# Expert weights that come turned, split beside the first experts, and bias rows made ahead of the last queries

## The chip, the cores and the metric

One core of a Trainium2 chip runs the whole kernel. The metric is device time in microseconds, the median of several executions. TensorE (PE) multiplies and transposes, VectorE (DVE), ScalarE (ACT) and GpSimd (POOL) work on elements, SyncE (SP) issues most transfers. Each engine takes its own instructions in order and waits on semaphores for the others.

## What is computed

Four batches of 512 rows of 128 go through two layers, with a residual after each part:

```python
x = x + L0_xattn(ctx, ctx, layernorm(x))      # 16 heads, features exp(z), exp(-z), 77 keys
x = x + L0_ffn(layernorm(x))                  # 8 experts of 64, top 2 of 8, and a shared one
x = x + L1_xattn(layernorm(x), ctx, ctx, mask)   # one head of 128, masked softmax over 77 keys
x = x + L1_ffn(layernorm(x))                  # 8 experts of 512, top 2, gelu(gate) * up, down
```

In the last part `gu = einsum('th,efh->etf', x, gate_up_w)` with `gate_up_w` of shape (8, 1024, 128) and `out = einsum('etf,ehf->eth', h, down_w)` with `down_w` of shape (8, 128, 512). TensorE needs both with the contracted index on the partitions, so turned against the way they are stored.

## The kernel before, in words

Everything stays in SBUF between the parts. Tokens lie 128 to a tile, four tiles to a batch. The order of work is written out by hand for each engine; semaphores carry the counts.

**First attention.** A step `G` (0 to 15) is one batch and a group of four heads: `scores(G)` on TensorE, `Exp` on ScalarE (L1013), `values`, a transposition, `normalise` on DVE. Beside it run the maxima of the next batch: GpSimd rounds the queries into `qh` (`round_queries`, L386), TensorE multiplies them with `kb`, DVE reduces (`mx`, L573). The negated maxima are transposed, copied by ScalarE (`copy_mT0`, L959, for batch 0 into `mT0`; `copy_mT`, L963, into `mT`) and moved by SP into `qs` (L310, L314). `project(b)` multiplies the output of batch b with `fc_w` and adds a bias row through `onecol` and `b2s`, for which it waits on `pool_bias`. GpSimd builds these rows (L410 to L429: the selection `selGt` and `selG`, the zeroed gates `g3`, the bias split in `b2p`, `b2s`, `onecol`) after `round_queries(3, q)`.

**First experts.** `hidden(b, c)`, c = 0 to 4, makes four parts of the expert layer and the shared layer of batch b; ScalarE applies Gelu (L1043), `spread_gates` spreads the gates, DVE multiplies (`gated`, L692), `moe_out` sums into banks 5 and 6, DVE adds the residual and takes the statistics (L697, L516, L519). The gates: `gate_logits`, `gate_exp`, then on DVE `gate_scores`, `first_best`, `second_best`, `best_weights`, `gate_parts` (ends at L627), then `turn_gates` on TensorE and `copy_gates` (L684). Batch 0 and batch 1 have gates of their own, batches 2 and 3 one chain together. A normalisation is `layernorm_stats`, `layernorm_rstd` on GpSimd (L364, L365) and `layernorm_apply` (L528).

**Second attention.** `scores1(b)`, `softmax_shift` on DVE (L748, L751, L754), `softmax_exp` (L1070), `turn_probs`, `copy_probs` (L1084), `values1`, `attention1_out` on DVE (L767 to L770 and statistics), a normalisation, `turn_xn3`, `expert_logits`. It starts after `moe_out(3)`. Between these, the weights of the second experts are turned: for each expert SP loads `upn` and `dnn` (L323, L324; the first three when the first attention is over, the rest as the ring of three comes free), `turn_weights(e)` transposes 12 blocks (L1507) into three banks, ScalarE copies two into `uphi`, rounded for a fast multiply, and one into `dnT` (L1066), and DVE subtracts the rounded part from the bank into `uplo` (`low_weights`, L762).

**Second experts.** Routing, then 39 blocks of 128 rows in a loop: a gathered block is multiplied with `uphi`, `uplo` and again `uphi` (L1139), Gelu, product, transposition, `down`. TensorE waits for `dve_upT` before it.

Of the kernel before, what the change touches and what calls it, by code (L numbers as in the profile page):

```python
# [16 lines left out]
P = 128  # L17
# [10 lines left out]
WR = 3  # L28
# [45 lines left out]
def two_layer_kernel(nc, A, out):  # L74
    with ExitStack() as ctx:
# [54 lines left out]
        g3 = sb("g3", [P, NT, 3, GR], BF16)  # L130
        g3r = sb("g3r", [P, NT, E0])


        l0 = ExitStack()
# [19 lines left out]
        mT0 = sb("mT0", [GH, NG, SEQ], at=l0)  # L154
        selGt = sb("selGt", [3 * E0, 3, 4 * P], BF16, at=l0)
# [29 lines left out]
        upn = sb("upn", [P, WR, 8, D])  # L185
        dnn = sb("dnn", [P, WR, F1])
        uphi = sb("uphi", [P, E1 * 2 * F1], F32R)
        uplo = sb("uplo", [P, E1 * 2 * F1], F32R)
# [39 lines left out]
        XT2 = (0, 1, 7, 1)  # L228
        XT3 = (5, 5, 5, 1)
        UPT = (2, 3, 0)  # L230
# [27 lines left out]
        pe_upT, act_upT, dve_upT = sem("pe_upT"), sem("act_upT"), sem("dve_upT")  # L258
# [31 lines left out]
        def _(sp):  # L290
# [16 lines left out]

            for g in range(NG):
# [8 lines left out]
            sp.wait_ge(dve_on, STEPS)  # L317
            sp.wait_ge(act_onT, NB * NI)
            sp.wait_ge(pool_mask, 1)
            for e in range(E1):  # L320
                if e >= WR:
                    sp.wait_ge(pe_upT, 3 * (e - WR + 1))
                sp.dma_start(upn[:, e % WR, :, :], A["L1_ffn_gate_up_w"][e].rearrange("(c f) h -> f c h", f=P)).then_inc(ld_up[e], 16)  # L323
                sp.dma_start(dnn[:, e % WR, :], A["L1_ffn_down_w"][e]).then_inc(ld_dn[e], 16)  # L324

# [20 lines left out]
        def _(g):  # L346
# [59 lines left out]
            for q in range(NG):  # L406
                round_queries(3, q)
# [17 lines left out]
            for t in range(3):  # L425
# [4 lines left out]
                .then_inc(pool_bias, 1)  # L430
            g.wait_ge(ld_mask, 16 * NB)
# [71 lines left out]
        def _(v):  # L503
# [178 lines left out]
            def copy_gates(b):  # L682
                v.wait_ge(pe_gT, b + 1)
                v.tensor_copy(gT3[:, b, :], bank[7 if b else 5].bitcast(BF16)[0:BR, 0:SEQ]).then_inc(dve_gT, 1)  # L684
# [15 lines left out]

            normalise(STEPS - 2)
# [15 lines left out]
            layernorm_apply(1, 3)  # L717
            copy_gates(1)
# [18 lines left out]
            layernorm_apply(2, 1)  # L737
            moe_out(3)
            layernorm_apply(2, 2)


            def softmax_shift(b):
# [5 lines left out]
                step(v.tensor_tensor(s, bank[4 + b % 2][:, 0:NI * KEYS].rearrange("p (i k) -> p i k", i=NI),  # L748
# [7 lines left out]

            def low_weights(e):
                for c in range(2):
                    n = 2 * e + c
                    cols = slice(n * SEQ, (n + 1) * SEQ)  # L760
                    v.wait_ge(act_upT, 3 * e + c + 1)
                    v.tensor_tensor(uplo[:, cols], bank[UPT[c]], uphi[:, cols].bitcast(F32), ALU.subtract).then_inc(dve_upT, 1)  # L762

# [977 lines left out]
```

## Time and profile before

| | us |
|---|---|
| median of 3 runs | 385.36 |
| lowest, highest | 384.67, 389.5 |
| the profiled execution, its own time | 385.88 |
| its span, first to last instruction | 384.1 |
| busy: PE, DVE, ACT, POOL | 304.9, 219.4, 161.3, 149.6 |
| chain that ended last: PE, DVE, POOL | 60%, 22%, 7% of the span |
| mean granted TensorE clock | 0.907 |

All rows are of one execution, in microseconds from the span's start. In a row of a timeline the first number is the start, the second how long the instructions were busy; x4 says that four were merged; what stands in brackets is the idle time of the engine before the row and who ended it. A line such as L1139 can be that of a helper used by many places, so the tile names say which multiply it is. The granted clock is a share of 2.4 GHz: 0.50 is 1.2 GHz.

### The profile page before, as it was taken

The page shows a single profiled execution, that of the slowest core. Times are in us where ns is not written, and L with a number is a line of the kernel's source. Part 1 is how long each engine was busy: PE and PEld are TensorE (multiplying, and loading weights), DVE is VectorE, ACT ScalarE, POOL GpSimd, SP SyncE. Part 2 cuts the span into 40 slices and gives each one's busy share as a digit, 9 for nine tenths or more (in the row PEclk, how much of TensorE's full clock was granted, in tenths as well). Part 3 has the DMA queues.
Part 4 walks back from the last instruction along what each step waited for, and adds up shares of the span by engine and source line. Part 5 has one row for each costly group of instructions (what it writes and reads, how often), then busy time and mean ns, then how long its engine had stood idle before and what let it go on. Part 6 is the DMA issues. An engine that isn't in the chain of part 4 may idle for free.

```text
span 384.1 us, 6281 instructions
## 1 busy us (share of the span) xinstructions
PE 304.9 (79%) x1964; PEld 218.9 (57%) x1965; DVE 219.4 (57%) x709; ACT 161.3 (42%) x255; POOL 149.6 (39%) x192
## 2 busy tenths in 40 slices
PE   6889798199988679889978541489999999999910
PEld 2344353164446447547867441268888888898810
DVE  5676265062557956463889958735455455455406
ACT  4478577047463423130565302023444444344404
POOL 4945308840102200111102314446776766665320
PEclk9999899689999969999999855579999999999975
DMA  7200000000000340000345110011111111122046
GB/s 245 73 4 1 5 1 4 2 0 5 0 3 0 108 139 1 2 1 0 106 145 190 42 40 0 13 37 36 48 50 41 48 48 45 44 48 41 22 127 223
DMA packets 16952, 19.09 MB, mean 50 GB/s; under 512 B 2336, under 2 KB 11904, under 8 KB 16928
## 3 DMA queue, kind: packets, MB, share of 16 engines
q1 hardware_dynamic: 14432, 13.67, 11.2%
q0 software_dynamic: 2496, 5.12, 5.1%
q8 instruction: 13, 0.21, 0.2%
q14 instruction: 11, 0.09, 0.1%
HBM read 13.99 MB, written 4.65 MB: 49 GB/s over the span
## 4 chain that ended last, share of the span: by engine, by line
PE 60%; DVE 22%; POOL 7%; issue 4%; DMA 4%; ACT 3%; SPq 0%; POOLq 0%; DVEq 0%; ACTq 0%
PE ps L1139 49%; PE ps L1631 4%; DVE xn L528 3%; DVE stats L516 2%; DVE uplo L762 2%; POOL rstd L365 2%; PE ps L1241 2%; DMA dnT<-y_dram 2%; PE ps L1144 1%; PE ps L1606 1%; DVE x L770 1%; DVE mv L519 1%; POOL qh L386 1%; DVE mx L573 1%; ACT ex L1013 1%
## 5 line engine op out<-in xcount | busy, mean ns | idle before, releaser
L364 POOL TENSOR_SCALAR rstd<-mv 128x4 f32<-128x4 f32 x16 | 4.0, 251 | 121.7 <-DVE mv L519 121.7
L481 POOL DMA_INDIRECT y_dram<-yb,dst_row x39 | 38.4, 984 | 33.0 <-DVE yb L903 33.0
L475 POOL DMA_INDIRECT xg<-xn_dram,src_row x39 | 37.9, 973 | 17.0 <-PE ps L1606 9.5
L1107 ACT ACTIVATE gl<-ps 128x512 f32<-128x512 f32 x39 | 23.3, 597 | 47.1 <-PE ps L1139 47.1
L1013 ACT ACTIVATE ex<-ps 77x1024 f32<-77x1024 f32 x32 | 30.9, 1015 | 27.5 <-PE ps L1139 27.5
L1139 PE MATMUL ps<-dnT,hhT 128*128 x312 | 41.4, 276 | 0.6 <-DVE yb L903 0.6
L573 DVE TENSOR_REDUCE mx<-ps 128x4 f32<-128x308 f32 x64 | 27.8, 474 | 24.0 <-PE ps L1139 23.2
L1139 PEld LDWEIGHTS ps<-dnT,hhT 128*128 128x128 f32 x312 | 37.8, 192 | 4.1 <-issue 0.8
L1113 ACT ACTIVATE hhT<-ps 128x512 f32<-128x512 f32 x39 | 23.3, 598 | 31.3 <-PE ps L1631 31.3
L1139 PE MATMUL ps<-uphi,xghi 128*128 x78 | 34.9, 448 | 0.9 <-DVE xghi L889 0.5
L889 DVE CAST xghi<-ps 128x128 fp32r<-128x128 f32 x39 | 11.4, 291 | 38.0 <-PE ps L1606 38.0
L1139 PE MATMUL ps<-uplo,xghi 128*128 x78 | 31.2, 400 | 0.0
L1139 PE MATMUL ps<-uphi,xglo 128*128 x78 | 31.2, 400 | 0.0
L897 DVE TENSOR_TENSOR hh<-gl,ps 128x512 f32<-128x512 f32 x39 | 26.4, 678 | 5.4 <-ACT gl L1107 5.4
L1139 PE MATMUL ps<-xnT,pack 32*128 32x512 f32 (+2 forms) x80 | 25.1, 598 | 1.6 <-ACT hraw L1043 1.0
L1139 PEld LDWEIGHTS ps<-kb,qh 128*128 128x128 f32 x64 | 10.5, 192 | 23.5 <-DVE mx L573 10.9
L1631 PE MATMUL ps<-ident,hh 128*128 128x128 f32 x156 | 23.5, 273 | 0.1
L939 ACT ACTIVATE xnT<-ps 128x512 f32<-128x512 f32 x16 | 9.5, 597 | 31.8 <-PE ps L1144 31.8
L1139 PE MATMUL ps<-kb,qh 128*128 128x308 f32 x64 | 20.0, 376 | 2.6 <-DVE mx L573 1.5
L1043 ACT ACTIVATE hraw<-ps,pack 128x512 f32<-128x512 f32 x16 | 10.8, 686 | 26.3 <-PE ps L1139 18.8
L1139 PE MATMUL ps<-qs,kst 32*128 32x512 f32 x128 | 18.8, 656 | 2.1 <-ACT ex L1013 2.1
L903 DVE COPY yb<-ps 128x128 f32<-128x128 f32 x39 | 11.4, 291 | 15.9 <-PE ps L1139 15.8
(222 smaller groups left out, 640.8 us busy)
## 6 DMA issues: line engine op xcount, KB each, us to landing
upn<-in_L_ffn_gate_up_w_dram SPq DMA_DIRECT2D x8, 512.0 KB, 3.9
dnn<-in_L_ffn_down_w_dram SPq DMA_DIRECT2D x8, 256.0 KB, 4.1
dnT<-y_dram SPq DMA_DIRECT2D x4, 512.0 KB, 6.4
xn_dram<-xn SPq DMA_DIRECT2D x4, 256.0 KB, 2.3
out_dram<-x SPq DMA_DIRECT2D x4, 256.0 KB, 2.3
x<-in_x_dram SPq DMA_DIRECT2D x3, 256.0 KB, 3.5
xg<-xn_dram,src_row POOLq DMA_INDIRECT x39, 2.6
y_dram<-yb,dst_row POOLq DMA_INDIRECT x39, 2.3
```

The lines of the kernel that those rows point to most:

```text
L475: g.indirect_dma_start(xg[:, k % XR, :], None, xn_dram, bass.IndirectOffsetOnAxis(ap=src_row[:, k:k + 1], axis=0)).then_inc(gathered[k % X ...
L481: g.indirect_dma_start(y_dram, bass.IndirectOffsetOnAxis(ap=dst_row[:, k:k + 1], axis=0), yb[:, k % 2, :], None).then_inc(scattered[k % 2] ...
L528: v.tensor_scalar(xn[:, b, i, :], x[:, b, i, :], mv[:, b, i, 0:1], rstd[:, b, i:i + 1], ALU.subtract, ALU.mult).then_inc(dve_xn, 1)
L573: v.tensor_reduce(mx[:, b % 2, i, GH * g:GH * g + GH], bank[4 + n % 2][:, 0:GK].rearrange("p (j k) -> p j k", j=GH), AX.X, ALU.max).then_i ...
L889: v.tensor_copy(xghi[:, s, :], bank[7][:, 0:P]).then_inc(dve_xg, 1)
L897: v.tensor_tensor(hh[:, s, :], gl[:, s, :], bank[2 + s], ALU.mult).then_inc(dve_h, 1)
L903: v.tensor_copy(yb[:, s, :], bank[6][:, 0:D]).then_inc(dve_y1, 1)
L1013: s.activation(ex[0:KEYS, p % RING, :, :], ps[0:KEYS, 2 * h:2 * h + 2, :], ACT.Exp, scale=SCALE).then_inc(act_ex, 1)
L1107: s.activation(gl[:, s_, :], bank[s_], ACT.Gelu).then_inc(act_gl, 1)
L1113: s.activation(hhT[:, s_, :, :].rearrange("p c t -> p (c t)"), bank[4], ACT.Copy).then_inc(act_hT, 1)
L1139: return pe.matmul(out_, lhsT, rhs, start=start, stop=stop, skip_group_check=True)
L1631: ins = pe.transpose(bank[4][:, c * P:(c + 1) * P], hh[:, s, c * P:(c + 1) * P], ident[:, :])
```

## The change

The host lays the two weights out turned (`up`: 128 x 1024 per expert; `down`: the four 128-row blocks of an expert side by side). SP loads `up` straight into `uplo`, three experts after the shifts of batch 0 and of batch 1, two after those of batch 2, and `down` into `dnT` when the first attention is projected. `uplo` has a place of its own from the start; `mT0` and `selGt` share other tiles (`mT`, `g3`). ScalarE rounds `uplo` into `uphi`, two experts after each of the first three batches of the first experts and two beside the first transposed rows of the second attention; DVE subtracts in place. The transpositions of weights, their copies and the ring are gone. The first scores and shift of the second attention are put before the last `moe_out`. The gates of batch 1 are worked out in pieces between the products of batch 0, before the last residual of the first attention. GpSimd rounds the last queries after the bias rows.

```diff
             for g in range(NG):
                 sp.wait_ge(act_mT, g + 1)
-                sp.dma_start(qs[FD:P:R, 0, g, :], mT0[:, g, :]).then_inc(shifted[0][g], 16)
+                sp.dma_start(qs[FD:P:R, 0, g, :], mT[0:GH, g % 2, :]).then_inc(shifted[0][g], 16)
+            for e in range(0, 3):
+                up_weights(e)
             for b in range(1, NB):
...
+                for e in range(3 * b, min(3 * b + 3, E1)):
+                    up_weights(e)
             sp.wait_ge(pe_fc, NB)
...
             for e in range(E1):
...
+                sp.dma_start(dnT[:, e * F1:(e + 1) * F1], A["down"][e]).then_inc(ld_dn[e], 16)
 # GpSimd
-            for q in range(NG):
-                round_queries(3, q)
             for part in range(3):
                 ordered(g.memset(selGt[:, part, :], 1.0))
...
                 .then_inc(pool_bias, 1)
+            for q in range(NG):
+                round_queries(3, q)
 # DVE, first experts
+            def low_weights(e):
+                cols = slice(2 * F1 * e, 2 * F1 * (e + 1))
+                v.wait_ge(act_hi, e + 1)
+                v.tensor_tensor(uplo[:, cols], uplo[:, cols].bitcast(F32), uphi[:, cols].bitcast(F32), ALU.subtract)\
+                    .then_inc(dve_lo, 1)
             gated(0, 0)
+            gate_scores(1, NI, 2 * NI)
+            first_best(NI, 2 * NI, r_s, 0, r_o1)
             gated(0, 1)
             attention_out(2)
+            second_best(NI, 2 * NI)
             gated(0, 2)
+            best_weights(NI, 2 * NI)
             gated(0, 3)
             layernorm_apply(1, 2)
-            gate_scores(1, NI, 2 * NI)
-            first_best(NI, 2 * NI, r_s, 0, r_o1)
+            gate_parts(NI, 2 * NI)
             attention_out(3)
-            second_best(NI, 2 * NI)
-            best_weights(NI, 2 * NI)
-            gate_parts(NI, 2 * NI)
+            copy_gates(1)
             layernorm_apply(1, 3)
-            copy_gates(1)
...
+            layernorm_apply(2, 0)
+            low_weights(0)
+            low_weights(1)
             moe_out(1)
-            layernorm_apply(2, 0)
             copy_gates(3)
             for c in range(4):
                 gated(3, c)
+            layernorm_apply(2, 1)
+            low_weights(2)
+            low_weights(3)
             moe_out(2)
...
+            softmax_shift(0)
+            layernorm_apply(2, 2)
+            low_weights(4)
+            low_weights(5)
+            moe_out(3)
+            softmax_shift(1)
+            layernorm_apply(2, 3)
+            attention1_out(0)
+            softmax_shift(2)
+            layernorm_apply(3, 0)
+            attention1_out(1)
+            softmax_shift(3)
+            layernorm_apply(3, 1)
+            attention1_out(2)
+            layernorm_apply(3, 2)
+            attention1_out(3)
+            layernorm_apply(3, 3)
+            low_weights(6)
+            low_weights(7)
 # ScalarE
+            def high_weights(e):
+                cols = slice(2 * F1 * e, 2 * F1 * (e + 1))
+                s.wait_ge(ld_up[e], 16)
+                s.activation(uphi[:, cols], uplo[:, cols].bitcast(F32), ACT.Copy).then_inc(act_hi, 1)
...
+                if b < NB - 1:
+                    high_weights(2 * b)
+                    high_weights(2 * b + 1)
...
+            copy_xT(2, 0, bank[0])
+            high_weights(6)
+            copy_xT(2, 1, bank[0])
+            high_weights(7)
+            softmax_exp(0)
+            copy_probs(0)
+            copy_xT(2, 2, bank[0])
+            softmax_exp(1)
+            copy_probs(1)
+            copy_xT(2, 3, bank[0])
...
 # TensorE
             hidden(1, 0)
+            turn_gates(1)
             pe.wait_ge(dve_x, NB - 1)
             transpose_xn(1, EARLY, bank[0])
             hidden(1, 1)
-            turn_gates(1)
+            spread_gates(1, 0)
             hidden(1, 2)
+            spread_gates(1, 1)
...
+                if b == NB - 1:
+                    pe.wait_ge(act_lg, EARLY + 1)
+                    transpose_xn(2, 0, bank[0])
                 moe_out(b - 1)
...
+            scores1(0)
+            turn_xn2(1)
+            moe_out(NB - 1)
+            scores1(1)
+            turn_probs(0)
+            turn_xn2(2)
+            scores1(2)
+            values1(0)
+            turn_probs(1)
+            turn_xn2(3)
+            scores1(3)
+            values1(1)
+            turn_xn3(0)
+            turn_probs(2)
+            values1(2)
+            turn_xn3(1)
+            expert_logits(0)
+            turn_probs(3)
+            values1(3)
+            turn_xn3(2)
+            expert_logits(1)
+            turn_xn3(3)
+            expert_logits(2)
+            expert_logits(3)
...
 # host
+    up = a["L1_ffn_gate_up_w"].transpose(0, 2, 1)
+    down = a["L1_ffn_down_w"].transpose(0, 2, 1).reshape(E1, 4, P, D).transpose(0, 2, 1, 3).reshape(E1, P, 4 * D)
```

## Rows read from the trace of the kernel before

**Rows 1.** Timeline of PE, 40 to 98: start us, us, engine line op, names, shapes
```profile
75.70 1.20 PE L1139 MATMUL ps<-pack,onT 128*128 128x128 f32 x4 [8.43 <-POOL onecol L429]
```

**Rows 2.** Timelines of POOL, 0 to 60, 55 to 80 and 180 to 225
```profile
14.62 0.70 POOL L378 TENSOR_TENSOR kb<-kst,pack 128x308 fp32r<-128x308 f32 x1
...
58.23 2.28 POOL L386 CAST qh<-qs 128x512 fp32r<-128x512 f32 x4 [16.59 <-ACT qs L955]
...
75.10 0.19 POOL L429 TENSOR_TENSOR onecol<-onecol,identb 96x1 bf16<-96x1 bf16 x1
...
202.19 1.04 POOL L365 TENSOR_TENSOR rstd<-rstd,neghalf 128x4 f32<-128x4 f32 x1
```

**Rows 3.** Busy us by stretch: PE, PEld, DVE, ACT, POOL, granted clock, DMA share, GB/s
```profile
76.00:80.00 4.00, 4.00 (x20) 3.63 (x19) 0.00 (x0) 0.00 (x0) 3.74 (x2) 0.50 0.02 4
132.00:137.00 5.00, 0.32 (x3) 0.32 (x4) 4.45 (x27) 0.63 (x1) 1.26 (x2) 0.81 1.12 361
...
184.00:221.30 37.30, 28.11 (x221) 24.74 (x222) 33.60 (x113) 20.87 (x39) 7.48 (x15) 0.94 0.40 127
...
221.00:225.00 4.00, 3.96 (x20) 3.78 (x18) 0.22 (x2) 0.60 (x1) 1.72 (x9) 0.50 0.21 80
```

**Rows 4.** Timelines of PE, 120 to 160 and 160 to 192
```profile
136.69 0.66 PE L1381 MATMUL ps<-identb,g 128*96 128x128 bf16 x4 [4.78 <-DVE g L627]
...
144.98 1.14 PE L1139 MATMUL ps<-pack,hg 128*128 128x128 f32 x8
...
154.45 1.02 PE L1139 MATMUL ps<-xnT,pack 128*128 128x512 f32 x2
...
167.66 0.61 PE L1139 MATMUL ps<-gT,selG 96*128 96x512 bf16 x2 [0.61 <-DVE gT L684]
...
177.88 1.13 PE L1139 MATMUL ps<-pack,hg 128*128 128x128 f32 x8 [0.43 <-DVE x L697]
...
191.06 1.09 PE L1139 MATMUL ps<-keyA,xnT 128*128 128x77 f32 x8
```

**Rows 5.** Timeline of DVE, 97 to 180, first experts
```profile
123.84 0.69 DVE L692 TENSOR_TENSOR hg<-hraw,ps 128x512 f32<-128x512 f32 x1 [1.71 <-PE ps L1139]
...
128.96 0.17 DVE L603 TENSOR_SCALAR r_s<-r_s 128x32 f32<-128x32 f32 x1
...
164.18 0.69 DVE L697 TENSOR_TENSOR x<-ps,x 128x512 f32<-128x512 f32 x1 [5.28 <-PE ps L1139]
```

**Rows 6.** Timeline of DVE, 180 to 226, second attention
```profile
184.19 0.69 DVE L697 TENSOR_TENSOR x<-ps,x 128x512 f32<-128x512 f32 x1 [4.06 <-PE ps L1139]
...
189.43 0.47 DVE L748 TENSOR_TENSOR sc<-ps,mask_i 128x308 f32<-128x308 f32 x1
...
199.07 0.17 DVE L767 RECIPROCAL srec<-ps 128x4 f32<-128x4 f32 x1
...
201.76 1.29 DVE L762 TENSOR_TENSOR uplo<-ps,uphi 128x512 fp32r<-128x512 f32 x2
203.26 1.11 DVE L528 TENSOR_SCALAR xn<-x,mv,rstd 128x128 f32<-128x128 f32 x4 [0.21 <-POOL rstd L365]
...
220.09 1.12 DVE L528 TENSOR_SCALAR xn<-x,mv,rstd 128x128 f32<-128x128 f32 x4 [0.47 <-POOL rstd L365]
224.99 0.29 DVE L799 TENSOR_REDUCE r_m<-ps 128x16 f32<-128x128 f32 x1 [3.78 <-PE ps L1139]
```

**Rows 7.** Timeline of DVE, 0 to 50
```profile
14.61 1.86 DVE L528 TENSOR_SCALAR xn<-x,mv,rstd 128x128 f32<-128x128 f32 x4
...
48.11 1.11 DVE L528 TENSOR_SCALAR xn<-x,mv,rstd 128x128 f32<-128x128 f32 x4
```

**Rows 8.** Groups of instructions, 184 to 221.3: busy us, mean ns | idle before
```profile
L762 DVE TENSOR_TENSOR uplo<-ps,uphi 128x512 fp32r<-128x512 f32 x16 | 10.3, 684 | 1.5 <-ACT uphi L1066 1.5
L1507 PE MATMUL ps<-ident,upn 128*128 128x128 f32 x64 | 8.9, 279 | 1.9 <-DVE uplo L762 1.8
L1066 ACT ACTIVATE uphi<-ps 128x512 fp32r<-128x512 f32 x16 | 8.9, 594 | 4.8 <-PE ps L1507 4.8
```

**Rows 9.** Timeline of SP's DMA queue
```profile
16.25 13.93 SPq L310 DMA_DIRECT2D qs<-mT  x4
39.80 52.27 SPq L314 DMA_DIRECT2D qs<-mT  x12
```

More of the change, by code:

```diff
@@ L27 @@
 E1, F1 = 8, 512
-WR = 3
 NT = NB * NI
@@ L683, in copy_gates @@
                 v.wait_ge(pe_gT, b + 1)
-                v.tensor_copy(gT3[:, b, :], bank[7 if b else 5].bitcast(BF16)[0:BR, 0:SEQ]).then_inc(dve_gT, 1)
+                v.tensor_copy(gT3[:, b, :], bank[7 if b >= 2 else 5].bitcast(BF16)[0:BR, 0:SEQ]).then_inc(dve_gT, 1)
             def gated(b, c):
@@ L747, in softmax_shift @@
                 s = sc[:, b % 2]
-                step(v.tensor_tensor(s, bank[4 + b % 2][:, 0:NI * KEYS].rearrange("p (i k) -> p i k", i=NI),
+                step(v.tensor_tensor(s, bank[1 + b % 2][:, 0:NI * KEYS].rearrange("p (i k) -> p i k", i=NI),
                                      maskb[:, b, :].rearrange("p (i k) -> p i k", i=NI), ALU.add))
@@ L755, in softmax_shift @@
                                        in1=s, op0=ALU.max, op1=ALU.subtract).then_inc(dve_s1, 1)
[L757 to L762, printed above, removed]
             def attention1_out(b):
@@ L958, in copy_mT0 @@
                 s.wait_ge(pe_nmT, g + 1)
-                s.activation(mT0[:, g, :], bank[7][0:GH, :], ACT.Copy, scale=-1.0).then_inc(act_mT, 1)
+                if g >= 2:
+                    s.wait_ge(shifted[0][g - 2], 16)
+                s.activation(mT[0:GH, g % 2, :], bank[7][0:GH, :], ACT.Copy, scale=-1.0).then_inc(act_mT, 1)
             def copy_mT(b):
                 s.wait_ge(pe_nmT, NG + b)
+                if b <= 2:
+                    s.wait_ge(shifted[0][NG - 1 if b == 1 else NG - 2], 16)
                 s.activation(mT[:, b % 2, :], bank[4][0:HEADS, :], ACT.Copy, scale=-1.0).then_inc(act_mT, 1)
@@ L1059, in _ @@
                         gate_exp(EARLY, EARLY * NI, NT)
-            def copy_weights(e):
-                for c in range(3):
-                    s.wait_ge(pe_upT, 3 * e + c + 1)
-                    cols = slice((2 * e + c) * SEQ, (2 * e + c + 1) * SEQ)
-                    dst = uphi[:, cols] if c < 2 else dnT[:, e * F1:(e + 1) * F1]
-                    s.activation(dst, bank[UPT[c]], ACT.Copy).then_inc(act_upT, 1)
+                if b < NB - 1:
+                    high_weights(2 * b)
+                    high_weights(2 * b + 1)
             def softmax_exp(b):
@@ L1070, in softmax_exp @@
                 s.activation(pr[:, b], sc[:, b % 2], ACT.Exp, scale=-SCALE).then_inc(act_s1, 1)
-            copy_xT(2, 0, bank[XT2[0]])
-            copy_xT(2, 1, bank[XT2[1]])
-            copy_weights(0)
-            copy_xT(2, 2, bank[XT2[2]])
-            copy_weights(1)
-            copy_xT(2, 3, bank[XT2[3]])
-            for b in range(NB):
-                softmax_exp(b)
             def copy_probs(b):
@@ L1083, in copy_probs @@
                     s.wait_ge(pe_o1, b - 1)
-                s.activation(prT[:, b % 2, :], bank[1][0:KEYS, :], ACT.Copy).then_inc(act_pT, 1)
-            copy_probs(0)
-            for b in range(NB):
-                if b < NB - 1:
-                    copy_weights(2 * b + 2)
-                    copy_probs(b + 1)
-                if b >= 1:
-                    copy_xT(3, b - 1, bank[XT3[b - 1]])
-                if b < NB - 1:
-                    copy_weights(2 * b + 3)
-            copy_xT(3, NB - 1, bank[XT3[NB - 1]])
+                s.activation(prT[:, b % 2, :], bank[3][0:KEYS, :], ACT.Copy).then_inc(act_pT, 1)
+            copy_xT(2, 0, bank[0])
[3 more added lines that the diff above has]
+            softmax_exp(0)
+            copy_probs(0)
+            copy_xT(2, 2, bank[0])
+            softmax_exp(1)
+            copy_probs(1)
+            copy_xT(2, 3, bank[0])
+            softmax_exp(2)
+            copy_xT(3, 0, bank[XT3[0]])
+            copy_probs(2)
+            softmax_exp(3)
+            copy_xT(3, 1, bank[XT3[1]])
+            copy_probs(3)
+            copy_xT(3, 2, bank[XT3[2]])
+            copy_xT(3, 3, bank[XT3[3]])
             s.wait_ge(dve_g, EARLY + 2)
@@ L1378, in turn_gates @@
                     pe.wait_ge(dve_gT, b)
-                dst = bank[7 if b else 5].bitcast(BF16)
+                dst = bank[7 if b >= 2 else 5].bitcast(BF16)
                 for i in range(NI):
@@ L1648, in block_step @@
                 turn_h(k - 1, 1 - s)
-            pe.wait_ge(dve_upT, 2 * E1)
+            pe.wait_ge(dve_lo, E1)
+            for e in range(E1):
+                pe.wait_ge(ld_dn[e], 16)
             turn_xg(0, 0, first=True)
```

111 lines of the change are left out of this document (19 added, 92 removed).

## The prediction

> **What bounds the kernel now.** I read the wait lists and the chain of waits first, then the stretches by engine, then the timelines around each wait. No one engine bounds the whole: there are stages, and the change touches three of them.
>
> Stage one is the hand-over from the second to the third batch of the first attention. TensorE stands idle for 8.43 us before its instruction at 75.70, released by GpSimd's `onecol` [rows 1]. GpSimd is late because its queue holds the fourth batch's queries ahead of the bias rows: it idled 16.59 us for them until 58.23, and only then built the selection and bias rows, which end at 75.10 + 0.19 = 75.29 [rows 2]. After the idle time TensorE's granted clock is 0.50 (1.2 of 2.4 GHz) from 76 to 80 [rows 3], so the projection also runs at half rate.
>
> Stage two is the gates of the first experts. TensorE waits 4.78 us, until 136.69, for DVE's last gate row of batch 1 [rows 4], while DVE's own queue held gaps earlier (1.71 us before 123.84) [rows 5].
>
> Stage three is the second attention, 184.19 (the last expert output is there) to 221.21 (end of the last normalised rows): 37.0 us [rows 6]. DVE is busy 33.60 of 37.30 us of it, TensorE at clock 0.94 for 28.11 [rows 3]. So DVE ends this stage; what it does not do itself it hardly waits for.
>
> **Bias rows ahead of the last queries.** GpSimd's work from 58.23 + 2.28 = 60.51 to 75.29 is 14.8 us [rows 2]. It moves into the gap before 58.23, which starts at 58.23 - 16.59 = 41.64. It would end at 41.6 + 14.8 = 56.4, 1.8 us before the queries come; they are not late. The small loads it needs were issued in the first ten microseconds. The mask conversion stays behind the queries, and is followed by slack. The wait before the projection goes: 8.43 us. The next releaser would be DVE or ScalarE data of that batch, and both had finished by 68. The projection took 4.3 us at clock 0.50; at full clock it is half, so another 2.2 us go. Together 10.6 us. What is late next is nothing new: the projection, then the chain scores, exponentials, values that stood there before.
>
> A cost stands against it. GpSimd now works beside DVE's normalisation of the fourth batch. At 14.61, beside a key spread of GpSimd at 14.62 [rows 2], four such DVE operations took 1.86 us, and at 48.11, beside nothing, 1.11 us [rows 7]. The one at 48.11 now falls among the GpSimd operations. DVE's next maxima release TensorE, so up to 0.75 us reach the path, at most twice that if a long operation is met; below nothing has no reason. I take 0.4 us, half of what the row shows, since TensorE has other work between.
> The Trainium skill, SBUF — State Buffer, section "Who interferes with whom", says why: one SBUF port pair serves both engines, and whoever starts second waits for the whole instruction. Its rule would also let the new low-part subtraction, which now has two SBUF inputs, block a GpSimd operation that reads SBUF. Here no GpSimd variance step falls beside one in my order of work, so by the rule the sum stays; no row here shows that pair.
>
> **Gates of batch 1.** From 121.45 DVE did the same work in another order. Scores and first best (2.0 us, from 128.96) [rows 5] now fill the 1.71 us gap. The third batch's residual and statistics, 2.0 us (as 184.19 to 186.17), move behind the gates. The last gate row then comes 1.7 + 0.2 + 2.0 = 3.9 us sooner, near 132.7 instead of 136.6. TensorE gains less: one transposition and one hidden-layer part, done before its wait, now stand behind it. Two such parts are busy 1.02 us [rows 4], start to start about 0.86 us each; four transpositions are busy 0.56 us by [rows 8], start to start 0.44. Together 1.3 us. So the first expert output, at 144.98 [rows 4], starts 3.9 - 1.3 = 2.6 us sooner. Bounds: 3.9 if all of it is covered, and 1.3 if the remaining wait of some 2.3 us still brings the clock down for as long as it stood at 0.50 after 76 [rows 3]; that halves part of 4 us, and 1.3 us more go.
>
> **Splitting the weights beside the first experts.** Nothing is saved in number of roundings: before, ScalarE rounded 16 pieces in 8.9 us and DVE subtracted 16 in 10.3 us [rows 8]; now there are 8 of twice the width each, by these rows at most the same sums: 1.1 us apiece on ScalarE and 1.3 on DVE (below that, what eight fewer starts save). They are hidden where they stand: two beside each expert output, where DVE idled 5.28 us before 164.18 [rows 5] (2.6 us of work plus 1.1 of normalising fit), two more in the wait for the fourth output, and the last two behind the last normalised rows, where DVE idles 3.78 us before 224.99 [rows 6]. Without that cover they cost 1.3 us each. ScalarE is idle over half of these stages. The transpositions vanish: 64 of the gate and up weights in 8.9 us [rows 8] and 32 of the down weights, with eight PSUM copies of ScalarE. They were not the bound of the stage, but DVE's subtraction was in its queue between the attention steps.
>
> One step is moved on to TensorE's path. Before moe_out(3) now stand the scores of batch 0 (0.86 us, eight at about 1.09 busy) [rows 4] and a transposition (0.44). Against them go the wait of 0.43 before 177.88 and most of the 0.61 before 167.66, since the fourth gate copy no longer stands behind a normalisation [rows 4]. Net 0.4 us lost; bounds 0 and 1.3.
>
> **The second attention.** New DVE work after the last expert output ends, in its order: residual and statistics 2.0; the shift of batch 1, three operations of 0.47 with gaps, 1.45; four attention outputs of 2.69 (199.07 to 201.76), 10.8; shifts 2 and 3, 2.9; the normalisation of batch 3 for the keys and four of the result, 1.1 each, 5.5 [rows 6]. The power of -1/2 on GpSimd takes 1.04 (202.19) [rows 2], and from the end of the statistics to the normalisation 1.5 us pass (201.76 to 203.26). For the first three normalisations a shift covers all but 0.1 us of it; for the last two nothing does, 3.0 us. Sum 2.0 + 1.45 + 10.8 + 2.9 + 5.5 + 0.3 + 3.0 = 25.9 us against 37.0: 11.1 us go. Of what goes, the subtractions are the larger part (14 of 16 stood in it unhidden); the rest are batch 0's shift and others done sooner and waits of before. TensorE needs some 3 us per batch, of DVE's 5.3, and ScalarE 1.6, so both keep up, even with TensorE at half clock. Bounds: 11.6, and 8.1 if TensorE's round through ScalarE (transposed probabilities, copy, values) is late by 1 us in three batches. What is late next is the variance step, in the last two batches.
>
> Routing, the loop of the second experts and the end stay: same instructions, same order. The loop's table of weights has only other addresses.
>
> **Sum.** -10.6 + 0.4 - 2.6 + 0.4 - 11.1 = -23.5 us. Against the profiled execution, 385.9 us (span 384.1), that gives 362.4. It stood 0.5 us above the median of the three runs, 385.4, so I predict 361.9 us.
>
> **Loads.** SP now issues three weight loads (1.5 MB) before the shift of batch 1's maxima at 39.80 [rows 9], which starts the scores. The queue moved 361 GB/s from 132 to 137 [rows 3]; 1.5 MB is then 4.4 us, and SP was free from 16.25 + 13.93 = 30.2 [rows 9]. No cost. The next five loads stand behind shifts.
>
> **Rivals.**
> Slower than before: the loads block the shifts. If packets of the turned weights moved slowly, scores of batches 1 and 2 would wait for a whole group. To eat the 23.5 us gained, 1.5 MB must take over 23.5 us beyond the shift, so under 67 GB/s; at 60 GB/s the time is 388. The 361 GB/s speak against it; only that the elements have another layout speaks for it. Chance 0.02.
> The first stage does not move: another wait (a late load, GpSimd work stretched past 61) takes the place of `onecol`. 361.9 + 10.2 = 372. Against it: 1.8 us of slack, and more before TensorE needs these queries. Chance 0.04.
> The split isn't hidden: 8 x 1.3 = 10.3 us come on to DVE's path, 372. Against it the gaps above. Chance 0.03.
> The second attention is bound by the TensorE and ScalarE round trip, since one bank serves each kind of transposition: half of its gain is lost, 361.9 + 5.6 = 367.5. For it: its instructions now alternate strictly. Chance 0.08.
> The clock stays up, in the gates stage and behind the last normalised rows (0.50 from 221 to 225 [rows 3], though the waits before it are now placed otherwise): 1.3 + 1.9 less, 358.7. Chance 0.10.
> It does not do what it says (both large terms fail): 381 to 385. Chance 0.01.
>
> **How the numbers follow.** The forecast has 0.72. Its bounds: gains of at most 10.6 + 3.9 + 0 + 11.6 and 1.9 of clock, 28.0, give 357.4; at least 9.1 + 1.3 - 1.3 + 8.1 = 17.2 give 368.2. With the neighbouring cases inside, the range is 357 to 368.5 and leaves out about 1 in 10. A measurement tells about 2% (7.7 us) from no change. Faster by over 2%: 0.97. Within: 0.01. Slower: 0.02.
>
> **What would show it.** Right: no wait on `onecol`, clock 0.9 or more through the projection; the turn of batch 1's gates some 4 us sooner relative to the first hidden layer; no transposition of weights; 25 to 27 us from the last expert output to the last normalised rows, in which DVE is busy over 80%, with two idle spots of 1.5 us on the variance. Wrong: SP or TensorE waiting on `qs` loads, DVE waiting on ScalarE's high parts, or TensorE waiting on ScalarE's probabilities for more than 1 us a batch.

## The result, and the profile after

| | before | after |
|---|---|---|
| median of 4 runs each, us | 385.58 | 361.94 |
| lowest, highest | 384.67, 389.5 | 360.91, 365.18 |
| the profiled execution, its own time | 385.88 | 360.91 |
| its span | 384.1 | 359.1 |
| mean granted TensorE clock | 0.907 | 0.903 |

The ratio is 0.938, with a 95% interval of 0.929 to 0.947. Forecast: 361.9 us, 357 to 368.5.

The page's first lines: busy time has fallen on TensorE (304.9 to 294.5) and hardly moved on DVE (219.4 to 219.9). TensorE's transpositions are gone; DVE does as much as before, at other places. (Line numbers in rows of after and of the experiments are those of that run's kernel.)

```profile
span 359.1 us, 6065 instructions
...
PE 294.5 (82%) x1868; PEld 210.4 (59%) x1869; DVE 219.9 (61%) x701; ACT 156.7 (44%) x239; POOL 151.4 (42%) x192
```

GpSimd's timeline, 40 to 62 (the counterpart of [rows 2]):

```profile
41.63 0.51 POOL L403 MEMSET g<- 24x512 bf16 x1
...
56.29 0.19 POOL L422 TENSOR_TENSOR onecol<-onecol,identb 96x1 bf16<-96x1 bf16 x1
59.06 2.28 POOL L381 CAST qh<-qs 128x512 fp32r<-128x512 f32 x4 [2.58 <-ACT qs L954]
```

The bias rows fill the gap and are done 2.6 us before the queries come. TensorE's timeline (the counterpart of [rows 1, 4]):

```profile
67.96 0.61 PE L1143 MATMUL ps<-pack,onT 128*128 128x128 f32 x4
...
122.71 0.42 PE L1385 MATMUL ps<-identb,g 128*96 128x128 bf16 x4 [2.00 <-DVE g L622]
...
131.32 1.14 PE L1143 MATMUL ps<-pack,hg 128*128 128x128 f32 x8
...
169.95 1.07 PE L1143 MATMUL ps<-keyA,xnT 128*128 128x77 f32 x8
```

The projection of batch 0 has no wait ahead of it, and its four multiplies take 0.61 us where they took 1.20. The gates of batch 1 still cost a wait, of 2.00 us in place of 4.78. Then DVE's timeline, 140 to 202 (the counterpart of [rows 5, 6]):

```profile
150.53 0.69 DVE L692 TENSOR_TENSOR x<-ps,x 128x512 f32<-128x512 f32 x1 [1.99 <-PE ps L1143]
...
157.99 2.35 DVE L699 TENSOR_TENSOR uplo<-uplo,uphi 128x1024 fp32r<-128x1024 f32 x2
162.77 0.69 DVE L692 TENSOR_TENSOR x<-ps,x 128x512 f32<-128x512 f32 x1 [2.43 <-PE ps L1143]
...
167.29 2.35 DVE L699 TENSOR_TENSOR uplo<-uplo,uphi 128x1024 fp32r<-128x1024 f32 x2
170.15 0.69 DVE L692 TENSOR_TENSOR x<-ps,x 128x512 f32<-128x512 f32 x1 [0.51 <-PE ps L1143]
...
189.44 1.11 DVE L523 TENSOR_SCALAR xn<-x,mv,rstd 128x128 f32<-128x128 f32 x4 [1.54 <-POOL rstd L360]
191.07 0.18 DVE L763 RECIPROCAL srec<-ps 128x4 f32<-128x4 f32 x1 [0.52 <-PE ps L1143]
...
195.34 1.11 DVE L523 TENSOR_SCALAR xn<-x,mv,rstd 128x128 f32<-128x128 f32 x4 [1.54 <-POOL rstd L360]
196.37 2.35 DVE L699 TENSOR_TENSOR uplo<-uplo,uphi 128x1024 fp32r<-128x1024 f32 x2
200.24 0.29 DVE L798 TENSOR_REDUCE r_m<-ps 128x16 f32<-128x128 f32 x1 [1.51 <-PE ps L1143]
```

Ahead of each output of the first experts (L692) DVE still waits after its subtractions, so these are hidden: 1.99, 2.43 and 0.51 us are left. The second attention is now 170.15 to 196.45, 26.3 us. The stretches (columns as in [rows 3]):

```profile
68.00:71.00 3.00, 3.00 (x29) 2.35 (x28) 1.52 (x3) 0.30 (x1) 0.00 (x0) 1.00 0.17 66
120.00:125.00 5.00, 2.44 (x12) 0.90 (x10) 4.69 (x23) 1.81 (x3) 0.26 (x2) 1.00 0.81 273
...
170.20:196.50 26.30, 19.51 (x111) 17.21 (x109) 21.73 (x91) 6.50 (x12) 7.33 (x15) 0.68 0.08 30
196.00:200.00 4.00, 4.00 (x20) 3.85 (x19) 2.73 (x4) 0.60 (x1) 3.54 (x8) 0.50 0.20 70
```

The ledger, from one profiled execution to the other; each row is the further change since the row above:

| point of the run | before | after | change | forecast |
|---|---|---|---|---|
| projection of batch 0 starts, with its clock | 75.70 (scores then at 80.13) | 67.96 (70.23) | -9.90 | -10.2 |
| first product of the first experts | 144.98 | 131.32 | -3.76 | -2.6 |
| last output of the first experts | 184.19 | 170.15 | -0.38 | +0.4 |
| end of the last normalised rows | 221.21 | 196.45 | -10.72 | -11.1 |
| first routing maximum | 224.99 | 200.24 | +0.01 | 0 |
| span | 384.1 | 359.1 | -0.25 | 0 |
| sum | | | -25.0 | -23.5 |

### The profile page after: what moved, and what is told of

Its sections match the earlier page's. It is cut to its first block, busy times and chain, and to the rows that moved or that the text cites. A ratio compares the mean times of both kernels' runs of the same rounds, so it can differ in the third digit from the quotient of the medians.

```text
span 359.1 us, 6065 instructions
## 1 busy us (share of the span) xinstructions
PE 294.5 (82%) x1868; PEld 210.4 (59%) x1869; DVE 219.9 (61%) x701; ACT 156.7 (44%) x239; POOL 151.4 (42%) x192
## 4 chain that ended last, share of the span: by engine, by line
PE 65%; DVE 22%; DMA 3%; issue 3%; ACT 3%; POOL 2%; SPq 0%; DVEq 0%; POOLq 0%; ACTq 0%
PE ps L1143 53%; PE ps L1613 5%; DVE xn L523 3%; DVE stats L511 2%; PE ps L1148 2%; DVE mx L568 2%; PE ps L1245 2%; PE ps L1588 1%; DMA dnT<-y_dram 1%; DVE hg L687 1%; DVE x L766 1%; DVE mv L514 1%; POOL rstd L360 1%; PE ps L1252 1%; DVE x L927 1%
## 5 line engine op out<-in xcount | busy, mean ns | idle before, releaser
L1143 PE MATMUL ps<-xnT,pack 32*128 32x512 f32 (+2 forms) x80 | 23.5, 577 | 1.5 <-ACT hraw L1051 0.9
L1143 PEld LDWEIGHTS ps<-kb,qh 128*128 128x128 f32 x64 | 10.6, 192 | 23.9 <-DVE mx L568 11.3
L1613 PE MATMUL ps<-ident,hh 128*128 128x128 f32 x156 | 23.5, 273 | 0.1
L523 DVE TENSOR_SCALAR xn<-x,mv,rstd 128x128 f32<-128x128 f32 x64 | 19.9, 378 | 5.8 <-POOL rstd L360 5.8
```

Source lines behind the costliest of these rows:

```text
L523: v.tensor_scalar(xn[:, b, i, :], x[:, b, i, :], mv[:, b, i, 0:1], rstd[:, b, i:i + 1], ALU.subtract, ALU.mult).then_inc(dve_xn, 1)
L1143: return pe.matmul(out_, lhsT, rhs, start=start, stop=stop, skip_group_check=True)
L1613: ins = pe.transpose(bank[4][:, c * P:(c + 1) * P], hh[:, s, c * P:(c + 1) * P], ident[:, :])
```

## Experiments

Every kernel was timed beside the kernel before, and ratios are to that. e1 to e4 ran on one chip, e5 to e8 on another, e9 to e12 on a third.

**e1_bias_alone: the kernel before with only GpSimd's order changed.**

```diff
-            for q in range(NG):
-                round_queries(3, q)
             for part in range(3):
...
                 .then_inc(pool_bias, 1)
+            for q in range(NG):
+                round_queries(3, q)
```

> The kernel before with one edit: the last queries are rounded after the bias rows. Theory (the wait on the bias rows was 8.43 us and its half clock 2.2 us of the path, and the work fits the gap with a loss of 0.8 us where GpSimd holds up DVE's normalisation): 10 us less than before, so about 375.5 us, no idle time on the bias rows, and the normalisation of the fourth batch about 2.4 us instead of 1.1. Rival (the time comes back later, because DVE or ScalarE of the next batch were as late): at most 3 us less, 382 or more.

376.09 us (before 385.9), ratio 0.975 [0.970, 0.981]. The term stands alone: span 374.1, 10.0 less (0.6 of it stood there from the first microseconds). The rival, 3 us at most, is out. The normalisation of the fourth batch took 3.41 us (at 46.02), more than the 2.4 that I expected.

**e2_queries_first: the kernel after with the two loops in their old order** (the same edit backwards).

> The changed kernel with the last queries rounded first again, all else changed. Theory: the 9.9 us that the first stage gained are given back and nothing else moves, so about 372 us and a span near 369; the normalisation of the fourth batch back to 1.1 us. Rival (the gains of the stages depend on each other, through loads or the clock): off that by more than 3 us.

373.75 us, ratio 0.966 [0.960, 0.973]: 11.8 above the kernel after's median. The old wait is back at its old size. TensorE, 70 to 78:

```profile
75.54 1.19 PE L1143 MATMUL ps<-pack,onT 128*128 128x128 f32 x4 [8.42 <-POOL onecol L424]
```

The gates wait is 2.00 us as in after, and from the last output to the routing it is 26.3 + 3.8 us. Up to the first product of the first experts the profiled execution is 10.0 us later than after (141.34 against 131.32), as expected. But its span, 373.2, is 14.1 above after's where I expected some 10: another 3.0 us came between that product and the next outputs, where the clock was 0.57 from 142 to 150 and after's was 1.00, and 1.0 us behind the routing. So by the span the rival's 3 us are passed, by the medians they are not; the first term is there at its full size, the 3.0 us are the clock's by the place where they arise, and what made the 1.0 stays open.

**e3_old_gates: batch 1's gates in their old order on DVE and TensorE.**

```diff
             gated(0, 0)
-            gate_scores(1, NI, 2 * NI)
-            first_best(NI, 2 * NI, r_s, 0, r_o1)
             gated(0, 1)
             attention_out(2)
...
             layernorm_apply(1, 2)
+            gate_scores(1, NI, 2 * NI)
+            first_best(NI, 2 * NI, r_s, 0, r_o1)
             attention_out(3)
+            second_best(NI, 2 * NI)
...
```

> The changed kernel with the gates of batch 1 in the order of before, on DVE and on TensorE. Theory: 3.8 us more than the changed kernel (the 13.66 us from the start to the first expert output, less the 9.9 of the first stage), TensorE waits about 4.8 us for the gates and runs at clock 0.50 behind it. Rival (the gain there came from the clock alone or from elsewhere): under 1.5 us more.

365.11 us, ratio 0.947 [0.942, 0.953], 3.2 above the kernel after. The wait is 4.77 us again, with four transpositions at half rate behind it (0.66 against 0.42):

```profile
126.30 0.66 PE L1385 MATMUL ps<-identb,g 128*96 128x128 bf16 x4 [4.77 <-DVE g L622]
```

The last output comes at 173.02, 2.9 us later than after. The theory of 3.8 was a little high, the rival (under 1.5) is out.

**e4_split_in_attention: all eight subtractions back between the steps of the second attention.** `low_weights(0)` to `low_weights(7)` go, one to two at a time, before each shift and each output of it.

> The changed kernel with DVE's eight subtractions moved back between the steps of the second attention, where they stood before; still no transposition of weights on TensorE and no copies of them on ScalarE. Theory (the stage is bound by DVE's queue): seven of the eight at 1.18 us come on to the path and one fills a wait of 1.54 us for the variance: 8.2 us more than the changed kernel, stage of 34 to 35 us instead of 26.3. Rival (the transpositions and their copies bound the stage): at most 2 us more.

369.43 us, ratio 0.957 [0.951, 0.962]. DVE's timeline:

```profile
174.50 0.69 DVE L692 TENSOR_TENSOR x<-ps,x 128x512 f32<-128x512 f32 x1 [2.78 <-PE ps L1143]
...
180.06 2.35 DVE L699 TENSOR_TENSOR uplo<-uplo,uphi 128x1024 fp32r<-128x1024 f32 x2
...
207.61 1.11 DVE L523 TENSOR_SCALAR xn<-x,mv,rstd 128x128 f32<-128x128 f32 x4 [1.55 <-POOL rstd L360]
```

The stage is 174.50 to 208.72, 34.2 us in place of 26.3: 7.9 us for eight subtractions of 1.18 (9.4), less the waits of after that they cover. The waits ahead of the outputs of the first experts are each 2.27 us longer than in after (4.26, 4.70 and 2.78), so the pairs of subtractions had been hidden there. That the stage begins 4.35 us later than after has other causes: 1.0 us stood there at the projection already (`xn` of batch 3 took 3.41 us), and 3.3 us were lost after the same 2.00 us wait for the gates, behind which the clock fell:

```profile
120.00:125.00 5.00, 3.00 (x18) 2.15 (x18) 4.69 (x21) 1.20 (x2) 0.00 (x0) 0.87 0.56 192
...
130.00:140.00 10.00, 9.89 (x55) 8.27 (x56) 7.12 (x28) 5.79 (x8) 0.00 (x0) 0.70 0.00 1
```

**e5_after_again: the kernel after on another chip**, beside e6 to e8.

> The changed kernel as it is, as the measure for the runs beside it: 361 to 363 us, span near 359 to 361, the stage of the second attention 26.3 us.

362.13 us (360.75 to 364.9), before 387.16, ratio 0.936 [0.929, 0.942].

**e6_dead_turns: TensorE's removed transpositions are put back**, 96 of them with nobody who reads them, eight groups of 12 among its steps in the second attention. The result of these is not used.

```diff
+            def dead(n):
+                for c in range(n):
+                    pe.transpose(bank[4][:, (1 + c % 3) * P:(2 + c % 3) * P], ident[:, :], ident[:, :])
...
             scores1(1)
+            dead(12)
```

> The changed kernel with 96 transpositions on TensorE put back into the second attention, of a constant block into a bank nobody reads: 10.6 us of TensorE's time at full clock, no copies. Theory (DVE's queue bounds the stage, TensorE has 3 of 5.3 us of work a batch): between 2.5 us less and 1 us more, less where the work keeps the clock up through the last turns and logits (3.8 us at clock 0.50 behind the last normalised rows). Rival (what the change gained there was TensorE's transpositions): 6 to 10 us more.

363.97 us, ratio 0.938 [0.932, 0.944]: 1.8 above e5. The stage is 28.3 us. The one wait of DVE on TensorE that they make is 2.53 us, early in it:

```profile
177.66 0.18 DVE L763 RECIPROCAL srec<-ps 128x4 f32<-128x4 f32 x1 [2.53 <-PE ps L1143]
```

The clock stands at 1.00 from 170 to 195 here, where after has 0.70; whether the kept clock pays for part of the work put back, no run shows. The 8.9 us of transpositions alone were not what the gain was made of, though they cost a little more than my upper expectation.

**e7_dead_turns_copies: e6 with 24 copies of 128x512 back on ScalarE** (three behind each probability copy and exponential; their result is not used either).

> As the run before, with 24 copies of 512 columns on ScalarE put back too (some 13 us of ScalarE's time), which nobody reads. Theory: at most 3 us more than with the transpositions alone, because single copies now stand ahead of a probability copy or a transposed row; ScalarE then has near 5 of 5.3 us a batch. Rival (ScalarE's copies bounded the stage): 8 us or more.

369.24 us, ratio 0.953 [0.949, 0.958]: 5.3 above e6, and I had expected 3 at most. DVE now waits twice, longer:

```profile
179.84 0.18 DVE L764 RECIPROCAL srec<-ps 128x4 f32<-128x4 f32 x1 [5.75 <-PE ps L1163]
...
189.27 0.18 DVE L764 RECIPROCAL srec<-ps 128x4 f32<-128x4 f32 x1 [4.10 <-PE ps L1163]
```

TensorE was itself waiting 2.3 us for ScalarE's `xnT` before each: copies in a queue that alternates strictly with TensorE hold up the chain, though ScalarE is busy only 18.4 of 35 us. The stage is 35.7 us, 7.4 more than in e6; from its end to the routing maximum it is 2.3 us in place of 3.8, at clock 1.00. My reading that what left ScalarE was free falls, for copies that stand where these do; the old ones stood at other places in the queue.

**e8_start_late: the first scores and shift of the second attention behind the last output**, as before the change.

```diff
-            scores1(0)
             turn_xn2(1)
             moe_out(NB - 1)
+            scores1(0)
             scores1(1)
```

> The changed kernel with the scores and the shift of batch 0 behind the last expert output instead of ahead of it. Theory: TensorE's last output ends 0.9 us sooner, DVE's shift of 1.45 us comes on to the path behind it, with a wait for the scores of up to 0.9: 0.5 to 1.5 us more. Rival (starting the attention early is what gained the larger part of the 10.7 us): 3 us or more.

368.02 us, ratio 0.952 [0.945, 0.959]. Expected were 0.5 to 1.5 above after; it is 5.9 above e5, so the rival (3 or more) came. The stage is 33.2 us. TensorE's first wait and what DVE then sees:

```profile
174.49 1.14 PE L1507 MATMUL ps<-ident,pr 128*77 128x128 f32 x4 [2.27 <-ACT pr L1074]
```

```profile
180.99 0.18 DVE L763 RECIPROCAL srec<-ps 128x4 f32<-128x4 f32 x1 [4.62 <-PE ps L1143]
```

With the 2.27 us wait the clock falls to 0.50, from 174 on; eight score multiplies take 1.99 us, in after 1.12 at the same place. With a batch's scores ready at the start, DVE waits for this chain once, for 0.52 us; without them it waits 4.62, 0.86 and 0.51 us.

**e9_bias_first: GpSimd makes the bias parts (L412 to L422) ahead of the selection rows**, so that `xn` of batch 3 meets shorter operations.

> The changed kernel with GpSimd building the bias rows (short operations of 0.2 to 0.4 us) ahead of the selection rows (0.5 to 1.15 us), so that other operations fall beside DVE's normalisation of the fourth batch. Theory (a DVE operation waits for the whole GpSimd operation beside it, so the loss goes with the length of these): the four normalisations take 1.6 to 2.0 us instead of 2.44, and the projection starts 0.3 to 0.6 us sooner. Rival (a fixed loss whenever GpSimd works): 2.4 us as before. The whole time moves by under 1 us either way.

361.93 us, ratio 0.940 [0.934, 0.945]: no gain, and `xn` got worse, against my expectation of 1.6 to 2.0 us. The edit did not put the short bias parts beside `xn`: they were over at 44.75, and beside `xn` stood selection rows. DVE's row in the timeline:

```profile
48.79 2.90 DVE L523 TENSOR_SCALAR xn<-x,mv,rstd 128x128 f32<-128x128 f32 x4
```

The same four by line L523, 48.7 to 51.7 (duration in ns of the shortest, the median and the longest), then GpSimd's timeline beside them:

```profile
L523 DVE TENSOR_SCALAR xn<-x,mv,rstd x4: 337/745/1314, 48.8 to 50.4; 128x128 f32<-128x128 f32 x4
```

```profile
49.10 0.60 POOL L352 TENSOR_SCALAR_AFFINE_SELECT g<-g 24x512 bf16<-24x512 bf16 x1
...
50.46 1.15 POOL L417 TENSOR_TENSOR g<-g 24x512 bf16<-24x512 bf16 x1
```

Two operations met one of 0.60 us each and took some 0.75; the last met the addition of 1.15 and took 1.31. So the theory, a loss that goes with the length, holds operation by operation, and the total of 2.90 does not speak against it. The projection starts at 69.16, 1.2 us later than in after; the clock was 0.59 from 40 to 48 here.

**e10_clock_kept: 83 dead transpositions in TensorE's gaps of the last three batches**, placed by the waits of the profile after (8, 8, 16, 5, 14 and 32), their result unused.

> The changed kernel with transpositions of a constant, read by nobody, in TensorE's gaps of the second half of the second attention (83 of them, none meant to be late for a real one). Theory (half clock there costs one wait of 0.5 us and half of the last turn and logits): clock 1.00 until the last normalised rows, the logits 1.5 to 2 us sooner, the last subtraction then ends the stage; 1.9 us less than the changed kernel. Rival (the clock is no part of it, or the added work is late): within 0.5 us, or slower.

359.12 us (358.75 to 359.98), ratio 0.934 [0.930, 0.938]:

```profile
180.00:196.00 16.00, 15.71 (x129) 14.21 (x128) 12.32 (x56) 3.32 (x6) 4.53 (x9) 1.00 0.14 51
196.00:200.00 4.00, 2.45 (x19) 2.12 (x18) 3.56 (x8) 0.91 (x2) 3.51 (x8) 1.00 0.17 66
```

The clock is 1.00 where it was 0.50. The stage itself is 25.7 us (0.6 less), and from the end of `xn` to the routing maximum 2.2 in place of 3.8. DVE ends the stage at either clock; the clock is worth something only where TensorE ends it, in the tail. By medians it is 2.8 us faster than e9 beside it, against the 1.9 that I expected of the clock.

**e11_late_clock_kept: e8 with 38 dead transpositions in its first two batches.** It asks how much of e8's 6.9 us is clock.

> The late start (scores and shift of batch 0 behind the last expert output), with such transpositions in TensorE's gaps of its first two batches. The late start took 6.9 us more in that stage than the changed kernel (33.2 against 26.3). Theory: 3.9 of them are the clock, which fell in the wait for the first probabilities, and 3.0 the order; so this one gives the stage 29 to 30 us. Rival (the order alone, through the round trip to ScalarE): 32 us or more.

366.84 us, ratio 0.951 [0.945, 0.958]. The stage is 173.75 to 203.46, 29.7 us: of the 6.9 us that a late start costs, 3.5 are the clock and 3.4 the order. The whole time shows only 1.2 us of it, because its runs range from 363.8 to 370.2; the profiled one, the longest, had a clock of 0.83 from 120 to 130 and 0.68 from 130 to 140, before the stage. The reading is therefore of the stage alone.

**e12_best: what the others taught, together.** e10's 83 dead transpositions; the subtractions (0, 1, 2), (3, 4, 5), (6, 7) ahead of the three last outputs and none in the tail; `xn` of batch 3 a step earlier; 16 dead transpositions ahead of the gates.

```diff
-                if g == 0 and b + 2 < NB:
-                    layernorm_apply(0, b + 2)
+                if G in (0, 3):
+                    layernorm_apply(0, 2 if G == 0 else 3)
...
-            turn_gates(1)
             pe.wait_ge(dve_x, NB - 1)
+            for c in range(16):
+                pe.transpose(bank[0][:, (c % 4) * P:(c % 4 + 1) * P], ident[:, :], ident[:, :])
+            turn_gates(1)
```

> The kernel after with four edits: xn of batch 3 goes into the step of DVE's maxima before (ahead of the row at 44.00, where DVE idles for 5.57 us), so that it no longer runs beside POOL's bias additions; 16 dead transposes fill TensorE's wait of 2.00 us for the gates of batch 1; the 83 dead transposes that kept the clock at 1.00 through the second attention and the tail (measured there: the last 3.79 us became 2.2); and all eight subtractions of the split stand ahead of the second attention (three, three and two beside the expert outputs), none in the tail. Theory: 1.33 us of xn goes, of which the path had kept 0.83; the tail is 2.2 us or a little less; the stretch of the attention stays near 25.7 or loses up to 1.2 us with the last two subtractions; and the runs that had lost the clock behind the gates no longer do, so the spread between runs (361 to 365) shrinks and the median is taken near 357.5 us, 356 to 358.5. Rival 1: the subtractions moved ahead of the attention push the last expert output back by what they take (two of them, 2.35 us), because the waits there hid only what was already placed: about 359 to 360, no better than the kernel that only kept the clock (359.1). Rival 2: the 2.00 us wait is not what the clock hangs on, and the runs spread as before.

357.84 us (356.51 to 361.73, 6 runs), before 386.8, ratio 0.926 [0.921, 0.931]. It is the fastest here: 4.1 below the kernel after's first measurement by medians, 1.3 below e10, whose interval it overlaps by 0.001. DVE, then the stretches:

```profile
37.82 3.90 DVE L523 TENSOR_SCALAR xn<-x,mv,rstd 128x128 f32<-128x128 f32 x4
...
43.26 0.86 DVE L568 TENSOR_REDUCE mx<-ps 128x4 f32<-128x308 f32 x2 [1.54 <-PE ps L1143]
45.17 0.86 DVE L568 TENSOR_REDUCE mx<-ps 128x4 f32<-128x308 f32 x2 [0.43 <-PE ps L1143]
...
65.02 0.87 DVE L568 TENSOR_REDUCE mx<-ps 128x4 f32<-128x308 f32 x2 [0.43 <-PE ps L1143]
...
168.72 0.69 DVE L692 TENSOR_TENSOR x<-ps,x 128x512 f32<-128x512 f32 x1 [0.51 <-PE ps L1143]
```

```profile
120.00:126.00 6.00, 5.17 (x22) 2.16 (x21) 4.41 (x17) 2.68 (x5) 1.27 (x2) 1.00 0.76 256
...
129.00:132.30 3.30, 3.30 (x16) 2.85 (x15) 2.90 (x12) 2.92 (x3) 0.00 (x0) 0.50 0.00 0
...
168.70:194.40 25.70, 23.75 (x194) 21.39 (x193) 21.61 (x90) 6.40 (x12) 7.27 (x15) 1.00 0.08 32
```

Four things follow. `xn` is still slowed, to 3.90 us, but 1.54 us of idle time are left after it, so it costs nothing. The projection starts at 64.96 against 67.96, of which 0.5 stood there from the first microseconds, so 2.5 us are gained where I had expected 0.8. Of these, 1.6 are not from `xn`: they are there at the maxima at 45.17, which in after come at 47.29, ahead of its `xn`. There the clock was 0.57 from 43 to 47 in after and 1.00 throughout in e12. The remaining 0.9 us are the clash. The subtractions ahead of the attention pushed no output back (DVE still waits 0.51 us before the last), so rival 1 is out. The stage is 25.7 us and the rest 2.2, both as in e10, where two subtractions still stood in the tail: to empty it gained nothing. And rival 2 holds: the wait for the gates shrank from 2.00 to 0.26 us, yet the clock fell to 0.50 at about 129 for some 3 us, after three microseconds in which TensorE had no gap, and the runs spread by 5.2 us as before. With a clock of 0.943 two runs took 356.5 and 356.6, with 0.920 one took 361.7.

## Why the prediction was right

**The bias wait** (-10.6 + 0.4; measured -9.90). Both halves came: the wait is gone, and the clock of the projection is 1.00. e1 and e2 show it as one independent cause. Within it the clash was under-sized. `xn` of batch 3 took 2.44 us beside two additions of GpSimd of 1.14 and 1.15, not the 1.86 of [rows 7]. DVE's maxima just ahead of it and the last ones before the projection, in before and in after:

```profile
47.33 0.86 DVE L573 TENSOR_REDUCE mx<-ps 128x4 f32<-128x308 f32 x2 [1.03 <-PE ps L1139]
67.17 0.86 DVE L573 TENSOR_REDUCE mx<-ps 128x4 f32<-128x308 f32 x2 [0.43 <-PE ps L1139]
```

```profile
47.29 0.86 DVE L568 TENSOR_REDUCE mx<-ps 128x4 f32<-128x308 f32 x2 [1.47 <-PE ps L1143]
48.07 2.44 DVE L523 TENSOR_SCALAR xn<-x,mv,rstd 128x128 f32<-128x128 f32 x4
...
68.02 0.86 DVE L568 TENSOR_REDUCE mx<-ps 128x4 f32<-128x308 f32 x2 [0.43 <-PE ps L1143]
```

From the one to the other pass 19.84 us in before and 20.73 in after, so the clash put about 0.9 us on the path, not 0.4 (0.7 by the start of the projection, 67.96 against 75.70 less 8.43). In e12, with no `xn` between them, 19.85 us pass: the 1.11 us that it took before cost nothing. My upper bound, "at most twice that if a long operation is met", held and for its reason: up to 1.5 us, and these additions are longer than the 0.70 of the key spread in [rows 2].

**The gates** (-2.6; measured -3.76 between the two profiles, 2.9 to 3.2 by e3). The term that was off is the 1.3 us for the work that "now stand behind" the wait. TensorE's restart came 4.1 us sooner (136.69 to 122.71, less 9.90), as the 3.9 for DVE's order said, and of these only 0.3 were lost up to the first product (8.61 us from the restart in place of 8.29). Part of this is the clock: it is 0.50 behind the 4.77 us wait of e3 and stayed at 1.00 behind 2.00 us in this execution. With the same order and a clock that fell behind the wait the way is 8.9 to 9.2 us (e4, e6, e11), so 0.6 to 0.9 are lost. How much of the 8.29 was half clock, and so what the moved work alone costs, stays open. The case of my lower bound (the clock still falls) came in e4, e6 and e11, and some us later in e2; with 1.3 us it was under-sized, for in e2, e4 and e11 it cost 3.0 to 3.4 up to DVE's first output of the first experts (139.99 in after), in e6 0.5.

**The split** (0; measured 0). Six of eight subtractions are followed by a wait of DVE for TensorE. The two in the tail stand in the 3.78 us as forecast. In the attention they cost 7.9 us (e4), 1.0 for each of 1.18.

**The scores before the last output** (+0.4; measured -0.38). Fewer waits between the products than I counted.

**The second attention** (37.0 to 25.9; measured 26.3). The addition of DVE's instructions and of two waits of 1.5 us is what the trace shows: 21.73 busy, 1.54 twice, and one wait of 0.52 on TensorE that I had left out. The forecast that TensorE at half clock keeps up holds as well, since the clock was 0.68 on average, and e10's full clock gains only 0.6. But the attribution was incomplete. I said that of what goes "the subtractions are the larger part" and the rest lesser things. Put back one at a time, the subtractions cost 7.9 us, the late start 6.9, the transpositions with copies, as e7 places them, 9.4, out of a total gain of 10.7. These are not parts that add up. Each would fill most of the stage's gain again, and the gain needed all three gone.

**The total.** The sum was 362.4 for the profiled execution, which took 360.91. It missed by 1.5 us, of which 1.2 are the gates and 0.8 the scores, and 0.25 the rest, against 0.3 and 0.4 the other way at the bias wait and the second attention. The median of after lies 1.0 above its profiled execution and that of before 0.3 below, so the median was met more closely than the sum deserves. None of the rivals came whole. The full clock behind the gates, a part of the fifth, did in the profiled execution, and its tail at full clock came only with dead transpositions (e7, e10, e12).

**The loads** cost nothing, as said. SP issues the three early ones between 30.2 and 31.6, and waits for the shift at 39.7 as before.

## What to carry to other kernels

Forecast a stage by adding the instructions and latencies of the engine that ends it, in its order. Then ask of every other queue whether it alone would fill the stage; such causes don't share the gain, each can hold most of it (6.9 to 9.4 of 10.7 us here). Put a small operation that another engine slows into an idle gap with room for the operations that it will meet there (1.11 us became 3.90 in e12), not ahead of work that releases TensorE. Where TensorE ends a stretch and its clock is 0.50 from gaps before, dead multiplies in these gaps can pay.

## What the runs showed of the hardware that I had not expected

**In a run of short DVE operations each can wait for a whole GpSimd operation.** Four normalisations of 128x128 take 1.11 us alone. Beside GpSimd operations they took 2.44 (after), 2.90 (e9), 3.39 (e10), 3.41 (e1, e4) and 3.90 us (e12). The price goes by how many are met and by how long each is: a single one of the four took 0.75 us beside an operation of 0.60 (e9), 1.31 beside one of 1.15 (after, e9) and 2.31 beside one of 2.26 (e12).

The reverse case, which no row of before showed, is in after. GpSimd, 195 to 199, beside DVE's two subtractions at 196.37, and e4 with nothing beside it at that operation and a subtraction beside the other:

```profile
196.62 2.26 POOL L455 TENSOR_SCALAR_AFFINE_SELECT before<-before 128x64 f32<-128x64 f32 x1
```

```profile
176.60 1.19 POOL L359 TENSOR_SCALAR rstd<-mv 128x4 f32<-128x4 f32 x1 [6.03 <-DVE mv L514]
...
208.88 0.29 POOL L455 TENSOR_SCALAR_AFFINE_SELECT before<-before 128x64 f32<-128x64 f32 x1
```

GpSimd waits for DVE's instruction: 2.26 us against 0.29, and 1.19 against the 0.23 of `rstd` in after. The Trainium skill, SBUF — State Buffer, section "Who interferes with whom", says that a DVE instruction with two SBUF inputs contends with a GpSimd one that reads SBUF; these rows agree. Four of e4's five variance steps of this stage stood beside a subtraction and took 1.19 to 1.20 us; in after, as the prediction said, none did, and all sixteen took 0.23 to 0.25.

**The same wait does not always bring the clock down.** Behind TensorE's 2.00 us wait for the gates the clock stayed at 1.00 in the profiled executions of after, e5, e7, e8, e9 and e10. It fell in those of e4, e6 and e11, and some 10 us later in that of e2. e12 filled the wait and the clock still fell some 9 us later, in a stretch where TensorE was busy throughout (its last gaps, 0.59 and 0.19 us, were before 122.04 and 125.83). In the first attention, too, it stood at half for some 3 us at different places: between 43 and 47 in after, between 51 and 55 in e1 and e10, nowhere in e12. After's slower runs are those with the lower mean clocks (360.91 and 360.95 at 0.903 and 0.906; 362.94 at 0.898; 365.18 at 0.895). That such falls, of 3.0 to 3.4 us where they were largest, make the spread of several microseconds between runs is likely, but only one execution of each kernel has a trace; what decides them stays open.
